# A row of masked weight sums, spread over the partitions by two transfers through DRAM instead of by identities, products and a copy

## The reference, cut to what matters

```python
def attn(data, weight, mask):              # mask: blocks of 32 x 32, on or off
    w_masked = weight * elem_mask
    return einsum('bsk,nk->bsn', data, w_masked)
def ffn(x, W_gate, b_gate, W_e, b_e):
    _, top_idx = top_k(x @ W_gate + b_gate, 2)
    y_all = relu(einsum('bsd,edh->bseh', x, W_e) + b_e)
    return take_along_axis(y_all, top_idx[..., None], axis=2).mean(axis=2)
x = x + attn(layernorm(x), weight, mask)
x = x + ffn(layernorm(x), W_gate, b_gate, W_e, b_e)
```

## Time and profile before

| | |
|---|---|
| median of 3 runs | 648.51 us |
| lowest and highest of them | 643.93 and 662.11 us |
| span of the profiled execution, first to last instruction | 641.3 us |
| mean granted TensorE clock | 0.991 |
| PE busy, share of the span | 625.5 us, 98% |
| PEld, DVE, ACT, POOL busy | 79%, 57%, 55%, 43% |
| share of PE in the chain that ended last | 92% |

### The profile page before, as it was taken

How to read it: one execution, slowest core, us unless ns; L and a number is a source line. 1 busy time by engine, 2 the same in 40 slices (tenths; PEclk the granted TensorE clock), 3 DMA queues, 4 the chain that set the end, 5 groups by cost and what they waited for, 6 DMA issues and landing times.

```text
span 641.3 us, 11277 instructions
## 1 busy us (share of the span) xinstructions
PE 625.5 (98%) x3495; PEld 507.8 (79%) x3498; DVE 368.2 (57%) x647; ACT 354.7 (55%) x434; POOL 273.0 (43%) x252
## 2 busy tenths in 40 slices
PE   6999999999999999999999999999999999999994
PEld 5676777788788888888888888888888888788884
DVE  5896597887877684455345146026224252399942
ACT  6776765676786534535434453543545447364663
POOL 2013211323556245554545355355454445464634
PEclk9999999999999999999999999999999999999996
DMA  8992875589876258988969959757999999866550
GB/s 347 408 407 87 317 273 190 182 322 330 293 236 251 114 184 222 291 196 215 254 179 228 228 169 223 204 148 193 269 207 230 252 244 234 223 108 118 83 86 2
DMA packets 89207, 140.25 MB, mean 219 GB/s; under 512 B 58304, under 2 KB 58304, under 8 KB 89152
## 3 DMA queue, kind: packets, MB, share of 16 engines
q1 hardware_dynamic: 25776, 92.85, 40.4%
q0 software_dynamic: 11376, 33.57, 23.8%
q10 hardware_dynamic: 52000, 13.11, 12.2%
HBM read 87.59 MB, written 46.14 MB: 209 GB/s over the span
## 4 chain that ended last, share of the span: by engine, by line
PE 92%; ACT 2%; DMA 2%; ACTq 1%; issue 1%; POOL 0%; SPq 0%; POOLq 0%; DVE 0%
PE psO L577 81%; PE psT L869 2%; PE psT L577 2%; PE psT L610 2%; PE psO L610 1%; PE psG L683 1%; DMA xb<-data_t 1%; ACTq L1215 1%; ACT x2T L1224 1%; DMA turned_odd<-x 1%; PE psS L664 1%; ACT xb L1264 1%; PE psT L651 0%; POOL rows_out L2032 0%; PE psT L695 0%
## 5 line engine op out<-in xcount | busy, mean ns | idle before, releaser
L577 PE MATMUL psO<-slots,xT 128*128 (+1 forms) x1728 | 397.3, 390 | 0.5 <-ACT psO L1168 0.4
L577 PEld LDWEIGHTS psO<-slots,xT 128*128 128x128 f32 x1728 | 322.9, 188 | 67.8 <-issue 1.7
L1588 DVE CAST slots<-raw 128x1024 fp32r<-128x1024 f32 x56 | 50.4, 899 | 187.0 <-DMA raw<-L_ffn_W_e 108.0
L577 PE MATMUL psO<-wT,xT 128*128 128x512 f32 x624 | 152.3, 397 | 0.0
L577 PEld LDWEIGHTS psO<-wT,xT 128*128 128x128 f32 x624 | 114.3, 188 | 25.1 <-issue 2.7
L1264 ACT ACTIVATE xb<-psO 128x512 f32<-128x512 f32 x72 | 43.0, 597 | 157.6 <-PE psO L577 119.1
L2015 POOL DMA_INDIRECT rows_out<-xb,tok_of x33 | 59.8, 1813 | 149.2 <-ACT xb L1264 131.2
L2009 POOL TENSOR_TENSOR xT<-x2T,xT 128x1024 fp32r<-128x1024 f32 x35 | 88.6, 2532 | 28.1 <-ACT xT L1232 15.8
L1590 DVE TENSOR_TENSOR slots<-raw,slots 128x1024 fp32r<-128x1024 f32 x56 | 74.8, 1337 | 1.9
L1168 ACT ACTIVATE psO<-bias_slot 128x512 f32 (+1 forms) x72 | 43.4, 602 | 41.6 <-issue 23.3
L1935 POOL TENSOR_SCALAR rs<-squares 128x1 f32<-128x1 f32 x16 | 8.7, 546 | 70.2 <-ACT rows_a L1017 40.6
(11 more groups left out here) (297 smaller groups left out, 638.0 us busy)
## 6 DMA issues: line engine op xcount, KB each, us to landing
raw<-L_ffn_W_e SPq DMA_DIRECT2D x56, 512.0 KB
x_rows<-x SPq DMA_DIRECT2D x16, 512.0 KB, 4.6
xb<-data_t SPq DMA_DIRECT2D x12, 512.0 KB, 4.7
mask_stage<-mask_blocks SPq DMA_DIRECT2D x8, 512.0 KB, 11.6
w_stage<-weight_t SPq DMA_DIRECT2D x8, 512.0 KB, 12.3
row_stage<-L_attn_weight SPq DMA_DIRECT2D x8, 512.0 KB, 11.2
xr<-L_attn_data SPq DMA_DIRECT2D x8, 512.0 KB, 6.2
x_planes<-planes_even SPq DMA_DIRECT2D x8, 512.0 KB, 3.1
```

The costliest lines, as they stand in the source:

```text
L577: last = eng.matmul(psum, xT[:, p, a, kt, :], moving(b, kt), start=(i == 0 and kt == 0 and not seeded), stop=(i == len(PASSES) - 1 and kt ...
L1588: eng.tensor_copy(slots[:, e % 2, HI, kt, :], raw[:, kt % 2, :]).then_inc(c_split, 1)
```

## The change

A tensor in DRAM, `sums_line`, of 1 x 1024 floats is added. Once all of `row_sum` is there, ACT issues `store_sums()`, a transfer that writes the 128 x 8 sums into that line, each float to its own place (element (p, r) goes to position 128 r + p, so that neither side is contiguous for more than one float). ACT then does `x_hi(4)` and `mean1(4)`, waits until the store has landed, and issues `spread_sums()`, a transfer that reads the line of 4 KB into each of the 128 partitions of `sum_row`. `correct` and `seed_mean` wait for this second transfer (`l_sums`) in place of `c_srow`. The eight scaled identities, the two products and the copy are gone, with the waits that guarded their buffers; `mean1(4)` now waits for the residuals of block 1 (`c_res`) before it overwrites `psT[:, 0]`.

```diff
+        sums_line = nc.dram_tensor("sums_line", (1, D), F32, kind="Internal").ap()
-            def row_of_sums(n):
-                eng.wait_ge(c_diag, PAIR * (n + 1))
-                eng.wait_ge(c_res, NH + n + 1)
-                eng.matmul(psT[:, 0, PAIR * n:PAIR * (n + 1), :].rearrange("p r n -> p (r n)"), ones[:],
-                           diagonals[:, PAIR * n:PAIR * (n + 1), :].rearrange("p r n -> p (r n)"),
-                           start=True, stop=True).then_inc(c_sums, 1)
...
                 if t == FIRST:
-                    eng.wait_ge(c_srow, 1)
+                    eng.wait_ge(c_res, 2 * NH)
...
-            def sum_diagonal(r):
-                eng.wait_ge(c_rows, r + 1)
-                eng.activation(diagonals[:, r, :], ident[:], ACT.Copy, scale=row_sum[:, r:r + 1]).then_inc(c_diag, 1)
-
-            def copy_sums():
-                eng.wait_ge(c_sums, NH)
-                eng.activation(sum_row, psT[:, 0, :, :].rearrange("p k t -> p (k t)"), ACT.Copy).then_inc(c_srow, 1)
+            def store_sums():
+                eng.wait_ge(c_rows, NT)
+                eng.dma_start(sums_line.rearrange("a (r p) -> p (a r)", p=P), row_sum[:], allow_slow_non_contiguous=True).then_inc(l_line, 16)
+
+            def spread_sums():
+                eng.wait_ge(l_line, 16)
+                eng.dma_start(sum_row, sums_line.rearrange("a d -> (a d)").partition_broadcast(P)).then_inc(l_sums, 16)
...
             def correct(t, n):
                 if n == 0:
-                    eng.wait_ge(c_srow, 1)
+                    eng.wait_ge(l_sums, 16)
```

More of the change, by code:

```diff
@@ L268, in build @@
         sum_row = raw[:, 1, :]
-        diagonals = bias_slot[:, 1, :].rearrange("p (r n) -> p r n", n=P)
         def tok_col(b):
@@ L330, in build @@
         c_masked, c_whi, c_rows = sem("c_masked"), sem("c_whi"), sem("c_rows")
-        c_diag, c_sums, c_srow = sem("c_diag"), sem("c_sums"), sem("c_srow")
+        l_line, l_sums = sem("l_line"), sem("l_sums")
         c_cor, c_sown, c_shift = sem("c_cor"), sem("c_sown"), sem("c_shift")
@@ L785, in _ @@
             project_pass(2, 1, 1)
-            row_of_sums(0)
             project_pass(2, 1, 2)
@@ L790, in _ @@
             project_pass(3, 0, 0)
-            row_of_sums(1)
             project_pass(3, 0, 1)
@@ L1053, in split_planes @@
                     eng.wait_ge(s_spare, 16)
-                elif t == 1:
-                    eng.wait_ge(c_sums, NH)
-                else:
+                elif t >= 2:
                     eng.wait_ge(l_planes[t % 2], 16 * (t // 2))
@@ L1094, in _ @@
             square1(1)
-            sum_diagonal(0)
-            sum_diagonal(1)
             x_hi(3)
-            sum_diagonal(2)
-            sum_diagonal(3)
-            sum_diagonal(4)
             mean1(2)
             square1(2)
-            sum_diagonal(5)
             mean1(3)
             square1(3)
-            sum_diagonal(6)
-            sum_diagonal(7)
+            store_sums()
             x_hi(4)
-            copy_sums()
             mean1(4)
+            spread_sums()
             fold_out()
```

## The result

The changed kernel is slower: 660.8 us in the median of 6 runs (655.76 to 663.59), against 644.25 us (641.64 to 662.11) for the kernel before in the same comparison. The ratio is 1.0237, 95% interval 1.0202 to 1.0272. The profiled execution has a span of 658.8 us, 17.5 us more than before. The forecast was 650.0 us and a range up to 657.5. The ratio is of undisturbed executions alone; in some others the granted clock is lower and the time over 1.5% longer, as in the one of 662.11 us above and in those that were profiled for experiments 3 and 9.

What follows compares the result with a forecast made beforehand. The prediction took TensorE, busy 98% of the span, as the bound: 641.3 - 1.81 + 3.3 = 642.8 us of span; the median lies 7.2 us above its span, so 648.5 + 1.5 = 650.0 us, range 643.8 to 657.5.

Steps and rivals of the forecast that it cites:

- What is removed, 1.81 us: On TensorE's chain: the two products between groups of 8 matmuls go, saving 0.92 + 0.89 = 1.81 us.
- The store, 5.5 us: ACT's transfer of the sums to DRAM, issued at about 48.5 us, lands 5.5 us later, at 54.0 us.
- The bounds of 2.6 and 14.7 us: For the store's landing: low from a quiet 512 KB store, high from a 4 KB load behind a full queue.
- the prediction's own formula, landing minus 57.0: Whole-kernel change in time equals the landing of the row minus 57.0 us, never less than -1.81.
- The issue, nothing: ACT's issue of the 1024-piece store lies in a gap of ACT's list, so nothing is added.
- The spread, 4.5 us: ACT's second transfer, 128 rows of 4 KB, takes 4.5 us with issue; row there at 58.5 us.
- VectorE, 4.6 us to the end of fold_parts: VectorE, blocked at correct(0, 0) until the row at 58.5 us, takes 4.6 us more, ending at 63.1.
- The stall, 3.3 us: TensorE's weight load at the gate's column sums waits from 59.86 to 63.15 us for fold_parts: 3.3 us.
- fold_out() would bind only if the store landed after 57: ACT's fold_out() comes at about 56 us; TensorE's transposes need it just before 58, so no cost expected.
- Rival (b), the clock: The TensorE stall brings its clock to 1.2 GHz, costing 4 to 6 us more: about 655.0 us; chance 0.18.
- Rival (c), the slow store: Single-float writes wait for one another, 20 us in all: change of +16, 664.5 us; chance 0.05.
- "Behind this place TensorE has no gap to its end": After the column sums nothing can recover the 1.5 us loss, so the span after 70 us is simply shifted.

Runs made afterwards that it cites:

- experiments 3: The changed kernel with both transfers issued by SyncE instead of ScalarE; ratio to the kernel before 1.0139.
- 9: The kernel before plus only the store of 1024 single floats on ScalarE's queue, nobody on TensorE's path waiting; ratio 1.0139.
- Experiment 6: The changed kernel with both transfers on SyncE and work reordered so TensorE needs nothing behind the row before 70 us; ratio to the kernel before 0.9986.
- experiment 16: The changed kernel reordered off TensorE's path, sums transposed and stored as 8 rows of 512 bytes, both transfers on SyncE; ratio to the kernel before 0.9976.
- Experiment 11: The changed kernel with sums turned by one TensorE transpose and stored as 8 rows of 512 bytes; ratio to the kernel before 1.0141.
- Experiment 2: The kernel before with VectorE held ahead of correct(0, 0) by five operations of 1.2 us, no transfer; ratio 1.0143.
- experiment 14: The kernel before plus two small loads on ScalarE's queue, 18 packets per engine, that no one waits for; ratio 1.014.
- experiment 10: The kernel before plus sixteen small loads on ScalarE's queue at block 9, 144 packets per engine; ratio 1.0139.
- Experiments 1: The kernel before plus the store and the spread on ScalarE's queue into a free buffer, nobody on TensorE's path waiting; ratio 1.0107.
- 13: The kernel before plus one small load on ScalarE's queue, 9 packets per engine, nobody on the path waiting; ratio 1.0098.
- 15: The changed kernel plus six small loads on ScalarE's queue, one each in blocks 8 to 13, 128 packets per engine in all; ratio to the kernel before 1.0137.
- 12: The changed kernel with the store as 8 rows of 512 bytes, reordered off TensorE's path, transfers on ScalarE's queue; ratio to the kernel before 1.0101.
- 8: The changed kernel run again, unchanged; ratio to the kernel before 1.0166.
- experiments 4: The changed kernel reordered so TensorE needs nothing behind the row before 70 us, transfers still on ScalarE; ratio to the kernel before 1.0123.

## Why the prediction was wrong

The direction was right; the time was 10.8 us too low, outside the range, and slower by over 2% had been given a chance of 0.06. The change itself was missed by more: +1.5 us was forecast and +16.6 measured. The forecast stood on a median of three runs, 648.5 us, which is 4.3 us over that of all six (644.25), so luck took 4.3 us off the miss. By its own steps:

**What is removed, 1.81 us.** Right. Experiment 6 shows 1.8 us and experiment 16 1.4 us as soon as nothing waits, both counted from their own first matmul (16 with one transpose more on TensorE).

**The store, 5.5 us.** The step that failed first: it measured 10.0 us (9.8 to 11.5 in the other runs). Of its 1024 pieces most are moved from 50.8 to 53 us and the last starts at 56.5, at some 9 ns of an engine each, less than the 24 ns taken, yet the landing is at 58.4; so the price isn't in the engines' busy share, from which the estimate was made. Experiment 11 shows what it hangs on: eight rows of 512 bytes land in 3.4 us. It changes the number of the pieces and their size together, so which of the two counts is open. (In `row_sum` the eight sums of a partition lie next to each other; it is the side in DRAM that breaks the store up.) The Trainium skill, "DMA: Bandwidth & Descriptors", "Rules for kernel authors", has one descriptor for every element of such a store, and the trace agrees: 1024 pieces of 4 bytes. That pieces under 512 bytes are read, modified and written ("Specifications") is shown by no run here. The 2.7 us worked out from its table of loads was a quarter of what was measured. The bounds of 2.6 and 14.7 us did hold it, and the prediction's own formula, landing minus 57.0, gives +5.7 with the row at 62.7, near the first stage's +7.3. The range's upper end was cut short of what the bounds gave, but their full +11 (659.5 us) would not have reached 660.8 either.

**The issue, nothing.** Right: 0.42 us in a gap of ScalarE.

**The spread, 4.5 us.** Right: 4.2 us.

**VectorE, 4.6 us to the end of fold_parts.** Right: 62.69 to 67.28.

**The stall, 3.3 us.** The mechanism was right, at L792 and released by fold_part; with the late row it is 5.8. VectorE's start is past 62 us, the prediction's own sign of a store priced too cheap.

**fold_out() would bind only if the store landed after 57.** It landed at 58.4, and bound: 1.1 us at the transposes. The sentence that the stall at L802 ends later anyway holds: the load there stands 5.7 us later, just what the formula gives with the row at 62.7.

**Rival (b), the clock.** Happened, as it was told, but cheaper: 3.7 us of work at 1.2 GHz lost 1.6 us where 5 were given. Experiment 2 shows it without any new transfer, 2.4 us for 5.8 us of work. It should have stood in the sum and not beside it, even for the 3.3 us of the forecast: in experiment 14 a stall of 3.2 us in the second stage brought the clock to 0.50 for 3.4 us, while one of 2.7 us in experiment 10 left it up. The row for 630 to 632 us was misread: TensorE has 68 matmuls there and is busy for 1.82 of 2 us, so they are tiny but not few, and the row shows no idle engine. The Trainium skill, "TensorE: Matmul & The Clock Gate", section "HAM oscillation — how this bites in real kernels", tells of waits between bursts of matmuls that put the array back to half its clock, and the trace agrees: 0.50 behind the stall of 5.8 us.

**Rival (c), the slow store.** Wrong in its size: 10, not 20 us.

**"Behind this place TensorE has no gap to its end", so all is simply shifted.** The second step that failed, and the larger: with the 7.3 us of the first stage alone the time would be about 648.5 + 7.3 = 655.8, in the range (644.25 + 7.3 = 651.6 from the median of six). The 7.9 us of the second stage, and 2.3 beyond TensorE's last pass, were in no case: what two transfers on ScalarE's queue do to the transfers behind them had no term in the sum. I had read ScalarE's issues of transposing transfers as a price, 1.3 to 4.0 us, and not asked why they vary. That row holds 13 of the 25, every quick one among them; the other 12 take up to 7.4 us. In order of time the trace of before shows 1.3 to 1.5 us at every fourth from place 4 on. Experiments 1, 13 and 14 give this loss without the change (1 with a stall at 278 us besides), 15 the change nearly without this loss. The prediction had named this as a sign of being wrong altogether, that the span after 70 us is not simply shifted.

## What to carry to other kernels

A small transfer is priced by its pieces and its landing, not by its bytes or the queue's busy share: here turning the column into rows before it went to DRAM took the store from 10.0 to 3.4 us. Before adding a transfer to a queue that later carries transfers on TensorE's path, look at the durations of those later issues in order of time; if they come in turns, as here, try whether a small transfer ahead of them moves the turn; here another queue (experiments 6 and 16) and padding to a full turn (15) were remedies. And no long wait of TensorE goes into a sum at its length alone: here one of 5.0 us cost over 7.

## What the runs showed of the hardware

- A store of 1024 single floats to DRAM landed 9.8 to 11.5 us after its issue, the same 4 KB as 8 rows of 512 bytes after 3.1 to 3.5 us (experiments 11, 12 and 16). A spread of 4 KB to 128 partitions took 3.6 to 4.2 us, and 5.8 in experiment 1.
- ScalarE's issue of a transposing transfer of 2080 packets took some 1.5 us when the packets ahead of it on its queue were, by the count above, a multiple of 8 per engine, and else mostly 2 to 8 us. One load of 9 packets per engine, 200 us earlier, made the kernel 1.0098 times as long (1.0073 to 1.0123); eight made it 0.9968 (0.9935 to 1.0).
- TensorE idle for 5.0 to 5.8 us at the column sums (the changed kernel, experiments 2, 8 and 15): granted clock 0.50 for 6.8 us, 1.6 to 2.6 us lost on top of the stall. Behind the stalls of 3.2 to 4.9 us in the second stage it was 0.50 for 3.4 to 6.8 us; those of 2.1, 2.4 and 2.7 us (experiments 4, 1 and 10) left it at 1.00.
